# The gate projection of a gated feed-forward layer: from plain float32 products to exact float32r halves

## The reference

```python
def _L1_ffn_ref(x, w_gate, w_up, w_down):
    x = act_qdq(x)                              # one scale for the whole tensor, rounded to 16 bits
    up = act_qdq(x @ lpbq_dequant(w_up).T)      # 256 -> 768
    gate = act_qdq(x @ lpbq_dequant(w_gate).T)  # 256 -> 768
    sig = fixed_qdq_u16(jax.nn.sigmoid(gate))
    gate = act_qdq(gate * sig)
    o = act_qdq(gate * up)
    return o @ lpbq_dequant(w_down).T           # 768 -> 256
```

## Time and profile before

| what | value |
|---|---|
| median of 3 runs | 1388.59 us |
| lowest and highest run | 1387.4 and 1388.69 us |
| span of the profiled execution | 1382.0 us |
| median less span | 6.6 us |
| gate half on TensorE, first transpose to end of the last gate product | 1053.6 to 1144.2 us |

### The profile page before, as it was taken

The page is one execution under the profiler, slowest core; times in us unless marked ns, Lnnn a source line. Parts: engine busy times, 40 slices in busy tenths (PEclk is TensorE's granted clock), DMA queues, the critical chain, the costliest instruction groups (busy, mean ns, idle before and its releaser), DMA issues. The chain is left out here.

```text
span 1382.0 us, 21094 instructions
## 1 busy us (share of the span) xinstructions
PE 1284.0 (93%) x7272; PEld 635.7 (46%) x7272; DVE 977.2 (71%) x1703; ACT 839.3 (61%) x1453; POOL 502.6 (36%) x670
## 2 busy tenths in 40 slices
PE   9999799999999999999999999999998999950799
PEld 5566323334343343434545554555444444420587
DVE  5876598887878878786666788887743435987522
ACT  4455337776777767777565556556553437959432
POOL 4455200235344454434673433333330003639200
PEclk9999869999999999999999999999999999975899
DMA  8999674233424243342343643333110001316132
GB/s 288 376 339 325 230 176 111 82 87 93 124 68 127 78 122 105 93 124 75 99 133 94 197 121 101 93 99 109 33 32 16 1 0 73 155 70 250 57 95 91
DMA packets 88190, 170.74 MB, mean 124 GB/s; under 512 B 14867, under 2 KB 49431, under 8 KB 86551
## 3 DMA queue, kind: packets, MB, share of 16 engines
q1 hardware_dynamic: 87547, 168.16, 39.2%
q10 hardware_dynamic: 539, 1.26, 0.4%
HBM read 108.26 MB, written 60.31 MB: 122 GB/s over the span
## 5 line engine op out<-in xcount | busy, mean ns | idle before, releaser
L1329 DVE TENSOR_REDUCE b_neg_max<-b_score 128x1 f32<-128x512 f32 (+3 forms) x864 | 541.2, 663 | 177.6 <-PE b_score L877 93.5
L1102 ACT ACTIVATE b_probs<-b_exp 128x512 f32<-128x512 f32 (+1 forms) x864 | 463.3, 581 | 281.9 <-PE b_exp L901 281.0
L874 PE MATMUL b_score<-b_k_stack,b_q_stack 97*128 97x512 bf16 (+3 forms) x1024 | 356.2, 351 | 14.7 <-issue 8.8
L901 PE MATMUL b_exp<-b_q_stack,b_k_stack 100*128 100x512 bf16 (+3 forms) x1024 | 344.6, 342 | 6.4 <-ACT b_probs L1102 5.6
L922 PE MATMUL b_av<-b_probs,b_values 128*17 128x512 f32 (+3 forms) x2048 | 228.5, 518 | 3.7 <-POOL b_probs L1200 3.4
L874 PEld LDWEIGHTS b_score<-b_k_stack,b_q_stack 97*128 97x128 bf16 x1024 | 99.8, 98 | 250.7 <-DVE b_neg_max L1329 128.5
L901 PEld LDWEIGHTS b_exp<-b_q_stack,b_k_stack 100*128 100x128 bf16 x1024 | 100.1, 98 | 82.6 <-ACT b_probs L1102 24.9
L1200 POOL TENSOR_SCALAR_AFFINE_SELECT b_probs<-b_probs 128x512 f32<-128x512 f32 x96 | 61.7, 643 | 176.7 <-ACT b_probs L1102 176.2
L1208 POOL CAST b_max_parts<-b_neg_max 128x16 bf16<-128x16 f32 x64 | 12.9, 202 | 286.3 <-DVE b_neg_max L1329 284.1
L877 PE MATMUL b_score<-diag_qk,minus_big 128*128 128x128 bf16 x512 | 112.6, 220 | 0.0
L1756 POOL TENSOR_TENSOR f_hidden<-f_tmp,f_hidden 128x2048 int32<-128x2048 int32 x8 | 44.3, 5532 | 137.7 <-DVE f_tmp L1708 137.7
(11 more groups left out here) (212 smaller groups left out, 1821.4 us busy)
## 6 DMA issues: line engine op xcount, KB each, us to landing
b_q_stack<-s_q SPq DMA_DIRECT2D x384, 64.0 KB
s_k<-a_part_k SPq DMA_DIRECT2D x48, 256.0 KB, 3.3
b_k_stack<-s_k SPq DMA_DIRECT2D x61, 192.0 KB
s_up<-f_up SPq DMA_DIRECT2D x6, 1536.0 KB, 5.0
s_va<-a_va SPq DMA_DIRECT2D x16, 544.0 KB, 5.4
b_values<-s_va SPq DMA_DIRECT2D x16, 544.0 KB, 4.1
a_mask_q<-mask_in SPq DMA_DIRECT2D x8, 1024.0 KB, 8.2
b_k_stack<-s_k SPq DMA_DIRECT2D x61, 128.0 KB
```

Source lines behind the costliest of these rows:

```text
L874: mm = pe.matmul(o, q, KS[half][0:R_MAX, h, 0:w], start=True, stop=causal or not general)
L901: mm = pe.matmul(o, k, QS[half][0:NSTACK, h, q0:T], start=True, stop=not masked)
L1102: nc.scalar.activation(probs[kc][:, h0:h0 + m, q0:T], exp_bank[n % RINGS][:, 0:m * w].rearrange("p (h n) -> p h n", h=m), ACT.Exp).then_in ...
L1329: nc.vector.tensor_reduce(neg_max[u][:, qt, h0:h0 + m], score_bank[n % RINGS][:, 0:m * w].rearrange("p (h n) -> p h n", h=m), AX.X, ALU.ma ...
```

## The change

Both operands of the gate products are split into a high part (the value rounded to the type float32r) and the exact remainder, also float32r. The weight is split once, on GpSimd, in the last part of the attention phase: `gate_high` lies where part of the query tile was, `gate_low` takes the place of the whole weight. Each batch of x is split when it leaves the PSUM banks: ScalarE writes the high part, VectorE subtracts it from the bank for the remainder. The whole x is still written to `xT`, which the up half reads. Each product of the gate then consists of three: high weight with low x, low weight with high x, high weight with high x (low with low is left out). The hardware loop of this half is written out. The filler products ahead of the first transposes are now float32r products on 64 rows each (`pairs_busy`), and wait for the split weight.

```diff
+def pairs_busy(pe, psum, weights, moved, count):
+    for _ in range(count):
+        for r in range(2):
+            rows = slice(P // 2 * r, P // 2 * (r + 1))
+            pe.matmul(psum[r][:, :], weights[rows, 0, 0:P], moved[rows, 0, 0:T], start=True, stop=True)
...
+                if t == LAST + 1:
+                    pool.wait_ge(exp_full, exponents_through(LAST - G, TT - 1))
+                    ffn.split_gate(pool)
...
+    def split_gate(self, pool):
+        pool.wait_ge(self.copied, len(self.banks))
+        whole = self.turned_to["gate"]
+        self.nc.gpsimd.tensor_copy(self.gate_high[:, :, :], whole[:, :, :]).then_inc(self.gate_split, 1)
+        pool.wait_ge(self.gate_split, 1)
+        self.nc.gpsimd.tensor_tensor(self.gate_low[:, :, :], whole[:, :, :], self.gate_high[:, :, :].bitcast(F32), ALU.subtract).then_inc(self.gate_split, 1)
...
                     def turn_x(b, half):
                         pe.wait_ge(x_rounded, b + 1)
                         for c in range(DC):
-                            if not (known(b) and b < 1):
+                            if b > 0:
                                 pe.wait_ge((x_by_dve, x_by_act)[c], b)
+                                pe.wait_ge(x_rest, DC * (b - 1) + c + 1)
...
                     def gate(b):
-                        pe.wait_ge(x_by_act, b + 1)
-                        pe.wait_ge(x_by_dve, b + 1)
+                        half = b % 2
+                        pe.wait_ge(x_rest, DC * (b + 1))
                         for f in range(FC):
-                            if not (known(b) and b < 1):
+                            if b > 0:
                                 pe.wait_ge(gate_copied, FC * (b - 1) + f + 1)
-                            product(b, f, w_gateT, gate_full)
...
+                            terms = [(wt, x[half], c) for wt, x in ((gate_high, x_low), (gate_low, x_high), (gate_high, x_high)) for c in range(DC)]
+                            for n, (wt, x, c) in enumerate(terms):
+                                mm = pe.matmul(bank[f][:, :], wt[:, c, f * P:(f + 1) * P], x[:, c, :], start=(n == 0), stop=(n == len(terms) - 1))
+                            mm.then_inc(gate_full, 1)
...
                             spread_on_tensor(pe, bank[0], "x")
-                            keep_busy(pe, const, bank[1], 11)
+                            pe.wait_ge(weights.gate_split, 2)
+                            pairs_busy(pe, bank[1:3], gate_high, gate_low, 6)
...
                     def copy_x(b):
+                        act.wait_ge(x_turned, 2 * b + 1)
+                        nc.scalar.activation(x_high[b % 2][:, 0, :], turn[0][:, :], ACT.Copy).then_inc(x_halved, 1)
                         act.wait_ge(x_turned, 2 * b + 2)
-                        nc.scalar.activation(xT[:, bass.ds(b, 1), 1, :].rearrange("p a n -> p (a n)"), turn[1][:, :], ACT.Copy).then_inc(x_by_act, 1)
+                        nc.scalar.activation(x_high[b % 2][:, 1, :], turn[1][:, :], ACT.Copy)
+                        nc.scalar.activation(xT[:, b, 1, :], turn[1][:, :], ACT.Copy).then_inc(x_by_act, 1)
...
                     def copy_x(b):
-                        dve.wait_ge(x_turned, 2 * b + 1)
-                        nc.vector.tensor_copy(xT[:, bass.ds(b, 1), 0, :].rearrange("p a n -> p (a n)"), turn[0][:, :]).then_inc(x_by_dve, 1)
+                        dve.wait_ge(x_halved, b + 1)
+                        nc.vector.tensor_tensor(x_low[b % 2][:, 0, :], turn[0][:, :], x_high[b % 2][:, 0, :].bitcast(F32), ALU.subtract).then_inc(x_rest, 1)
+                        nc.vector.tensor_copy(xT[:, b, 0, :], turn[0][:, :]).then_inc(x_by_dve, 1)
+                        dve.wait_ge(x_by_act, b + 1)
+                        nc.vector.tensor_tensor(x_low[b % 2][:, 1, :], turn[1][:, :], x_high[b % 2][:, 1, :].bitcast(F32), ALU.subtract).then_inc(x_rest, 1)
```

More of the change, by code:

```diff
@@ L9 @@
 F32 = mybir.dt.float32
+F32R = mybir.dt.float32r
 BF16 = mybir.dt.bfloat16
@@ L1368, in __init__ @@
                     "down": flat[:, last - 2 * n:last - n].rearrange("p (c i) -> p c i", c=DC)}
-        self.turned_to = {"up": sb("w_upT", [P, DC, FF], F32), "gate": sb("w_gateT", [P, DC, FF], F32), "down": sb("w_downT", [P, FC, D], F32)}
+        self.turned_to = {"up": sb("w_upT", [P, DC, FF], F32), "gate": sb("w_gateT", [P, DC, FF], F32)}
+        self.gate_low = nc.alloc_sbuf_tensor_at("f_w_gate_low", [P, DC, FF], F32R, offset=nc.sbuf_base - DC * FF * 4)
+        self.turned_to["down"] = sb("w_downT", [P, FC, D], F32)
+        self.gate_high_at = const["stack_at"]
+        self.gate_high = nc.alloc_sbuf_tensor_at("f_w_gate_high", [P, DC, FF], F32R, offset=self.gate_high_at)
+        self.gate_split = const["sem"]("f_gate_split")
         self.magic = sb("magic", [P, 1], F32)
@@ L1453, in gated_ffn_phase @@
     MINE = 2
-    w_upT, w_gateT, w_downT = (weights.turned_to[n] for n in ("up", "gate", "down"))
+    w_upT, w_downT = (weights.turned_to[n] for n in ("up", "down"))
+    gate_high, gate_low = weights.gate_high, weights.gate_low
     magic, magic_set = weights.magic, weights.magic_set
@@ L1470, in gated_ffn_phase @@
         hidden = sb("hidden", [P, FC, NB, T], F32)
+        halves_at = nc.sbuf_base
         up = [sb(f"up{i}", [P, FC, T], F32) for i in range(2)]
         tmp = [sb(f"tmp{i}", [P, FC, T], F32) for i in range(2)]
+        assert nc.sbuf_base - 4 * (FC - 2) * T <= weights.gate_high_at <= nc.sbuf_base - 4 * DC * FF
+        x_high, x_low = ([nc.alloc_sbuf_tensor_at(f"f_x_{n}{i}", [P, DC, T], F32R, offset=halves_at + 4 * DC * T * (2 * k + i)) for i in range(2)]
+                         for k, n in enumerate(("high", "low")))
         order = ["x", "gate", "act", "up", "prod"]
@@ L1615, in up_step @@
                                 pe.wait_ge(up_copied, FC * (b - 1) + f + 1)
-                            product(b, f, w_upT, up_full)
-                    over_batches(pe, step)
+                            if b == 0 and f == 0:
+                                pe.wait_ge(x_by_act, NB)
+                                pe.wait_ge(x_by_dve, NB)
+                            up_product(b, f)
+                    for b in range(NB):
+                        step(b, b % 2)
                     gate(NB - 1)
@@ L1633, in copy_gate, with step @@
                             act.wait_ge(gate_full, FC * b + f + 1)
-                            nc.scalar.activation(hidden[:, f, bass.ds(b, 1), :].rearrange("p a n -> p (a n)"), bank[f][:, :], ACT.Copy).then_inc(gate_copied, 1)
-                    def step(b, half, k):
-                        if not known(b):
+                            nc.scalar.activation(hidden[:, f, b, :], bank[f][:, :], ACT.Copy).then_inc(gate_copied, 1)
+                    def step(b, half):
+                        if b > 1:
                             act.wait_ge(x_turned, 2 * (b - 1))
-                        shift(xi[half][:, :, :], normed[:, bass.ds(b, 1), :].rearrange("p a (t d) -> p (a t) d", t=TT), "x").then_inc(x_shifted, 1)
-                        if not (known(b) and b < 1):
+                        shift(xi[half][:, :, :], normed[:, b, :].rearrange("p (t d) -> p t d", t=TT), "x").then_inc(x_shifted, 1)
+                        if b > 0:
                             copy_x(b - 1)
-                        if not (known(b) and b < 2):
+                        if b > 1:
                             copy_gate(b - 2)
@@ L1677, in _ @@
                     wait_scale(act, "x")
-                    over_batches(act, step)
+                    for b in range(NB):
+                        step(b, b % 2)
                     copy_x(NB - 1)
@@ L1731, in _ @@
                     scale_on_vector(dve, bank[0], "x")
-                    over_batches(dve, step)
+                    for b in range(NB):
+                        step(b, b % 2)
                     copy_x(NB - 1)
```

26 lines of the change are left out of this document (14 added, 12 removed).

## The result

| kernel | median us | lowest to highest, runs | ratio to before, 95% interval |
|---|---|---|---|
| before | 1387.99 | 1383.9 to 1388.69, 4 | |
| changed | 1377.32 | 1370.92 to 1379.18, 4 | 0.9918 [0.9891, 0.9945] |

The change makes the kernel faster, by 10.7 us where 19.3 were forecast, and 1377.3 lies outside the range of 1366.5 to 1374.5. The profiled execution of the changed kernel is its quickest run, 1370.92 us, with a span of 1369.2.

The account below looks back on a forecast made before the run. TensorE was taken to bound the gate half. The span, 1382.0 - 20.3 (cheaper products) + 1.05 (later start) = 1362.7 us, with the profile's 6.6 us distance to the median gave 1369.3 us; 8-in-10 range 1366.5 to 1374.5.

Parts of the forecast that it names:

- What bounds the kernel: Last phase: TensorE, busy 93.52 of 95 us, ends the gate half; time saved there moves all that follows.
- The passes: Gate products on TensorE: a float32r product takes 0.2157 us, like bf16; six replace four float32 products per bank, saving 20.3 us.
- the rivals of a second pass or an uncovered load: Gate products hold TensorE longer than one pass: 1431 us with a second pass, 1424 with uncovered loads; joint chance 0.08.
- The weight load under a product: Gate products: even a 190 ns load hides under the product before, adding nothing; wholly uncovered it would cost 54.7 us.
- The start: Ahead of the first gate product: splitting x there is uncovered, so that product starts 1.05 us later, near 1057.4.
- the clock rival: Clock falls to half speed at the start or in the thinner feed: about 1371.5 us; chance 0.05.
- The split of x: Gate batches in steady state: extra ScalarE and VectorE work stays covered, with 1.7 us slack before the transposes; cost nothing.
- The split of the weight: GpSimd's idle 14.14 us late in attention: the split takes at most 8.4 us, ends by 1039.9 and costs nothing.
- the end of the gate half: VectorE's last reductions finish 2.8 instead of 2.4 us behind the last product; the 0.4 us is covered.
- The base: The profile stands 6.6 us under the runs' median; the same distance was added to the forecast span of 1362.7 us.
- the signs that the prediction set down for being wrong: Two records a product or spacing above 0.22; loads ending holes; clock below 1.00 after 1056; VectorE's subtraction releasing every batch's transposes.
- the chain rival: VectorE's chain becomes the gate half's pace: transposes wait 1 us a batch, 7 us in all, so 1376 us; chance 0.05.

Follow-up runs that it names:

- fill: The changed kernel with the constant bf16 filler restored (11 products) and six more fillers ahead of the second transposes; 1372.63 us.
- late30: The changed kernel with 30 instead of 24 filler products at the end of attention, nothing else; 1372.65 us.
- Cols256b: The changed kernel with each gate product made as two of 256 columns, all six terms of one half of a bank first; 1377.48 us.
- load64: The changed kernel with 64 of 128 weight columns in the middle four of each bank's six products; 1376.63 us.
- stride_w: The changed kernel with bf16 weights read at four-byte steps, dense bf16 x, and the constant filler of the kernel before; 1366.35 us.
- stride_x: The changed kernel with x read as bf16 at four-byte steps and dense bf16 weights; 1372.74 us.
- start: The changed kernel with 30 fillers ending attention, bf16 fillers at the start, and batch 0's first three banks of gate products ahead of the second transposes; 1371.09 us.
- start2: The kernel start timed again without an edit; 1370.7 us.
- before_b: The kernel before, unchanged, in a further execution; 1383.62 us.

## Why the prediction was right and wrong

**What bounds the kernel** was right: TensorE set the end of the gate half, the time saved before U moved all behind it, and U to the end stayed 238.0 us.

**The passes**: the kind was right and the size wrong. A product is one record, a float32 product two, and the rivals of a second pass or an uncovered load fell. The step that failed is "I take that for a float32r product. The four-byte moving operand is no reason for more". It costs 0.2343 us, not 0.2157: 288 x 0.0186 = 5.4 us, over 60% of the miss of 8.6 us. The argument rested on an "if": that a float32 record is two passes which each read the four-byte columns, 0.4295 / 2 = 0.2148 us each. A float32r product is slower than such a half, so the record's halves can't be priced as products of that type. The rest of the half matches: 288 x 0.2343 + 5.2 = 72.7 us from G to U, where fill and late30 have 72.79. Cols256b shows a rate per column, load64 and stride_w clear the weights, stride_x finds somewhat over half of the excess (56 to 58%) in the four-byte step of the moving operand alone. What the rest is, no run tells.

**The weight load under a product** was right at its 190 ns, and with more room than thought: loads overlap one another too.

**The start**: the term of 1.05 us was right as worked out (late30 has 1.01 more than before). The step that failed is the weight of the clock rival, 0.05, and in it the reading of the earlier trace rows as holes "as long". The stretch there held 1.86 us without TensorE, the first part of the hole ahead of A; the changed kernel had this hole of 2.17 us, 1.65 us of filler, and holes of 1.25 and 1.62 in a row. The clock fell in all three traces of the changed kernel, which costs 1.05 us in the first and 2.7 in the other two, and in none of the three of the kernel before. Over all kernels with the split x, it fell in nine of the ten traces with 2.17 us of hole ahead of A (not in stride_w) and in none of the three with 0.88 (late30, start, start2). That points at this hole, and isn't proof: late30 is the only trace with the short hole and the new filler, and its other runs have a lower mean clock. Nor does the hole act alone. Of the eight traces with the long hole and the new filler all have the fall; of the four with the long hole and the constant filler of the kernel before (before, before_b, fill, stride_w) only fill has it. So the new filler, which is shorter (1.65 us at the full clock against 2.54) and leaves 1.25 us idle behind it where the old one left 0.46, is a second suspect. No run exchanges the filler alone, and fill, where the fall came in the middle of the old filler, shows that the old one doesn't always prevent it. Which of the two carries the cost stays open.

**The split of x**: right, the transposes waited for VectorE in no batch behind the first two. One batch of VectorE in the changed kernel:

```profile
1077.09 3.35 DVE L1741 TENSOR_REDUCE f_tops_gate<-f_hidden 128x6 f32<-128x3072 f32 x1 [3.50 <-ACT f_hidden L1676]
1080.36 0.74 DVE L1582 TENSOR_SCALAR f_tmp<-f_tmp,f_scale_x 128x1024 f32<-128x1024 f32 x1
1081.02 0.68 DVE L1734 TENSOR_TENSOR f_x_low<-f_turnx,f_x_high 128x512 fp32r<-128x512 f32 x1
1081.62 0.68 DVE L1735 COPY normed<-f_turnx 128x512 f32<-128x512 f32 x1
1082.22 0.68 DVE L1737 TENSOR_TENSOR f_x_low<-f_turnx,f_x_high 128x512 fp32r<-128x512 f32 x1
```

Each instruction starts 60 to 80 ns before the record ahead of it ends, so the five take 5.8 us, not the 6.1 of the sum of their lengths, and VectorE idles 3.50 us a batch. Adding lengths overstates such a chain by a few per cent.

**The split of the weight** and **the end of the gate half**: right. The split took 5.0 us against a bound of 8.4, and U to the end didn't change.

**The base.** "The 6.6 us lie around it" was wrong: around each execution lie 1.65 to 1.8 us (1370.92 over a span of 1369.2), in every run whose span is listed beside its time. By that the profiled execution of before, span 1382.0, took about 1383.8 us, some 5 less than the median. That didn't spoil the sum, which took one difference off the median, but it hid the scatter, for which the range left 1 us: A lies from 1050.2 to 1053.6 in the three traces of the kernel before and its variant, and up to 1056.3 in those of the changed one. The kernel before runs from 1383.3 to 1392.3 us over all its runs, the changed one from 1370.9 to 1379.2.

Two of the signs that the prediction set down for being wrong came true, the spacing above 0.22 and the granted clock below 1.00 after 1056, and none of the others. That the median lies near the 1376 of the chain rival is chance: its mechanism, transposes that wait for VectorE, stands in no batch behind the first two.

In all: 19.3 forecast, less 5.4 for the spacing, less 1.05 to 2.7 for the clock, leaves 11.2 to 12.9. The traces have 93.7 - 82.6 = 11.1 to 93.7 - 80.9 = 12.8, and the medians 10.7, with an interval from 7.6 to 15.1 that holds these.

## What to carry to other kernels

A type that the trace doesn't show is to be priced with a range even where its number of passes is sure: 9% on a product, times 288, was more than every wait together. Where a change makes TensorE's holes longer, sum the holes on both sides of it and put in the half-speed case with its own price; here the traces with six more filler products at one place (late30, start, start2) don't have that cost. And cut every trace at two or three common instants before comparing spans, since 6 us of scatter ahead of the change can look like its cost; the granted clock by stretches, compared between two traces of one kernel, shows where such scatter arises.

## What the runs showed of the hardware

- A float32r product of 512 columns takes 0.2343 us, of 256 columns 0.118, and a bf16 one 0.2155, each with a 128-column weight load of its own: 0.454 ns a column, at the granted clock of 1.00.
- A bf16 product whose moving operand steps by four bytes takes 0.226 us; with stepped weights 0.2156.
- Load records of 188 ns follow one another every 118 ns; at 64 columns they are 135 ns long.
- Twelve float32r products of 64 rows, two by two on the two halves of the array, take 1.65 us in all, the length of some seven whole ones: the halves run side by side.
- With a hole of 2.17 us ahead of A the granted clock fell to 0.50 as early as 1.3 us behind A (fill, inside a filler without holes), as late as 6.1 us behind it (stride_x), or not at all (stride_w, before); with 0.88 us ahead, TensorE kept 1.00 while busy for 1.72 of 4 us (late30).
- The clock also fell in five traces between 1020 and 1024 us, in the last part of attention, where TensorE's longest hole is 0.5 us (in again it was busy for 3.74 of the 4 us from 1018 to 1022); each such fall cost 1.6 us. The same place stayed at 1.00 in the other eleven traces.
- Differences of up to 2.4 us in the first 36 us, and why the clock falls at one place in some executions only, stay open.
